# The last low part of h*y on VectorE between the residual adds, and sequence 0 projected bank by bank

## The reference

```python
x = L0_attn_x
xn = _layernorm(x, axis=-1)
x = x + _L0_attn_ref(xn, ...) + _L0_ffn_ref(xn, ...)

# _L0_attn_ref: a gated linear recurrence
y = gelu(xn @ w_y + b_y)
conv = causal 4-tap convolution over time of (xn @ w_x + b_x), plus conv_b
gate_x, gate_a = sigmoid(conv @ w_ig + b_ig), sigmoid(conv @ w_ag + b_ag)
a = exp(-8 * gate_a * softplus(a_param));  mult = sqrt(1 - a * a)   # 0 and 1 at t = 0
h[t] = a[t] * h[t-1] + gate_x * conv * mult
out = (h * y) @ w_out + b_out

# _L0_ffn_ref: ternary weights q(w) = clip(round(w / s), -1, 1) * s with s = mean(abs(w))
out = (silu(xn @ q(w1).T) * (xn @ q(w3).T)) @ q(w2).T
```

## Time and profile before

| | before |
|---|---|
| median of 3 runs | 72.7 us (72.6 to 72.8) |
| profiled execution | 72.7 us |
| its span | 70.9 us |
| TensorE matmuls busy | 67.0 us, 95% |
| VectorE busy | 56.5 us, 80% |
| ScalarE busy | 52.1 us, 73% |
| GpSimd busy | 42.4 us, 60% |
| granted TensorE clock | 1.00 |

### The profile page before, as it was taken

The page is one execution under the profiler, slowest core; times in us unless marked ns, Lnnn a source line. Parts: engine busy times, 40 slices in busy tenths (PEclk is TensorE's granted clock), DMA queues, the critical chain, the costliest instruction groups (busy, mean ns, idle before and its releaser), DMA issues.

```text
span 70.9 us, 1026 instructions
## 1 busy us (share of the span) xinstructions
PE 67.0 (95%) x327; PEld 56.2 (79%) x327; DVE 56.5 (80%) x100; ACT 52.1 (73%) x80; POOL 42.4 (60%) x57
## 2 busy tenths in 40 slices
PE   4999999999999999999999999999999999999940
PEld 4998898877888888888888888888888889987630
DVE  0098898999999999999939964198976999996660
ACT  3395798599989999999989768989969961333000
POOL 6577874799996591000000899678796698566300
PEclk9999999999999999999999999999999999999999
DMA  0899999999000000000000000000000000000564
GB/s 0 293 226 320 393 400 404 389 340 359 18 0 0 5 0 0 0 0 0 0 5 0 5 0 9 0 0 0 0 0 0 0 0 0 0 0 0 191 246 155
DMA packets 4021, 6.66 MB, mean 94 GB/s; under 512 B 476, under 2 KB 1456, under 8 KB 4016
## 3 DMA queue, kind: packets, MB, share of 16 engines
q1 hardware_dynamic: 3728, 6.46, 25.6%
q10 hardware_dynamic: 288, 0.14, 0.7%
HBM read 5.56 MB, written 1.05 MB: 93 GB/s over the span
## 4 chain that ended last, share of the span: by engine, by line
PE 66%; DVE 10%; POOL 5%; issue 5%; ACT 4%; DMA 4%; POOLq 2%; DVEq 0%
PE slot L790 26%; PE slot L773 24%; DVE slot L668 5%; PE slot L853 4%; PE slot L886 4%; DMA par<-params 4%; PE slot L821 3%; PE slot L799 3%; PE slot L762 2%; POOL rstd L271 2%; DVE slot L657 2%; POOLq L52 2%; POOL conv_lo L347 2%; ACT L462 2%; DVE tx L674 1%
## 5 line engine op out<-in xcount | busy, mean ns | idle before, releaser
L301 POOL TENSOR_TENSOR g_lo<-w_raw,g_hi 128x512 fp32r<-128x512 f32 x10 | 12.9, 1303 | 14.6 <-DVE tx L641 12.3
L790 PE MATMUL slot<-xt_hi,w_q 128*128 128x512 f32 x40 | 15.7, 393 | 0.0
L790 PE MATMUL slot<-xt_lo,w_q 128*128 128x512 f32 x40 | 15.7, 393 | 0.0
L629 DVE SCALAR_TENSOR_TENSOR w_raw<-w_raw,s,slot 128x512 f32<-128x512 f32 x10 | 7.4, 747 | 4.9 <-ACT w_raw L407 4.9
L607 DVE SCALAR_TENSOR_TENSOR conv<-slot,par,conv 128x511 f32<-128x511 f32 (+2 forms) x12 | 9.0, 748 | 0.4
L790 PEld LDWEIGHTS slot<-xt_lo,w_q 128*128 128x128 f32 x40 | 7.5, 188 | 1.7
L790 PEld LDWEIGHTS slot<-xt_hi,w_q 128*128 128x128 f32 x40 | 7.5, 188 | 1.7
L407 ACT ACTIVATE w_raw<-slot,scale 128x512 f32<-128x512 f32 x10 | 6.8, 689 | 2.4 <-PE slot L790 2.3
L811 PE MATMUL slot<-g_hi,w_q 128*128 128x512 f32 (+1 forms) x25 | 8.3, 346 | 0.0
L811 PE MATMUL slot<-g_lo,w_q 128*128 128x512 f32 (+1 forms) x25 | 8.2, 346 | 0.0
L293 POOL TENSOR_TENSOR conv_lo<-conv,conv_hi 128x512 fp32r<-128x512 f32 x4 | 5.9, 1473 | 1.5 <-ACT conv_hi L428 1.4
(11 more groups left out here) (127 smaller groups left out, 164.8 us busy)
## 6 DMA issues: line engine op xcount, KB each, us to landing
w_raw<-w13t SPq DMA_DIRECT2D x2, 682.0 KB, 7.4
w_raw<-dense SPq DMA_DIRECT2D x5, 256.0 KB, 5.5
x_both<-x SPq DMA_DIRECT2D x4, 256.0 KB, 4.0
x_both<-xt SPq DMA_DIRECT2D x2, 512.0 KB, 5.3
out<-x_both SPq DMA_DIRECT2D x3, 256.0 KB, 2.1
w_raw<-w2t SPq DMA_DIRECT2D x1, 640.0 KB
out<-x_both ACTq DMA_DIRECT2D x1, 128.0 KB, 2.0
out<-x_both SPq DMA_DIRECT2D x1, 128.0 KB, 1.7
```

Source lines behind the costliest of these rows:

```text
L301: nc.gpsimd.tensor_tensor(g_lo[:, j, s], g[:, n % RING], g_hi[:, j, s].bitcast(f32), ALU.subtract).then_inc(g_lo_set, 1)
L629: nc.vector.scalar_tensor_tensor(out=g[:, n % RING], in0=silu[:, n % RING], scalar=s32[:, 0:1], in1=slot[H_SLOT[s][j]][:, 1], op0=ALU.mult ...
L790: mm = nc.tensor.matmul(slot[H_SLOT[s][j]][:, o], w13_q[:, c, col:col + P], v[:, s, c], start=(c == 0 and v is xt_hi), stop=(c == KC - 1 a ...
```

## The change

GpSimd makes three of the four low parts of h*y, all but the last (sequence 1, chunk 1). That one is made by VectorE (`last_hy_lo`), between the residual adds 0 and 1, with a semaphore of its own, on which TensorE waits for the terms that read it. TensorE projects sequence 0 one bank after the other, as it does sequence 1: all six terms of bank 0, then all six of bank 1.

```diff
--- before.py
+++ after.py
@@ -180,7 +180,7 @@
             sem("h_psum"), sem("silu_set"), sem("g_set"), sem("g_hi_set"), sem("g_lo_set"))
         t_psum, silu_t_set, g_t_set, gt_hi_set, gt_lo_set = (
             sem("t_psum"), sem("silu_t_set"), sem("g_t_set"), sem("gt_hi_set"), sem("gt_lo_set"))
-        hy_hi_set, hy_lo_set = sem("hy_hi_set"), sem("hy_lo_set")
+        hy_hi_set, hy_lo_set, hy_lo_last_set = sem("hy_hi_set"), sem("hy_lo_set"), sem("hy_lo_last_set")
         o_psum, o_set = sem("o_psum"), sem("o_set")
 
         ON_ACT = FULL + 1
@@ -341,10 +341,10 @@
 
             for c in range(KC):
                 gated_products(c)
-            for s in range(SEQS):
-                for c in range(KC):
-                    pool.wait_ge(hy_hi_set, KC * s + c + 1)
-                    nc.gpsimd.tensor_tensor(hy_lo[:, s, c], tx[:, s, c], hy_hi[:, s, c].bitcast(f32), ALU.subtract).then_inc(hy_lo_set, 1)
+            for n in range(SEQS * KC - 1):
+                s, c = divmod(n, KC)
+                pool.wait_ge(hy_hi_set, n + 1)
+                nc.gpsimd.tensor_tensor(hy_lo[:, s, c], tx[:, s, c], hy_hi[:, s, c].bitcast(f32), ALU.subtract).then_inc(hy_lo_set, 1)
 
 
         @block.scalar
@@ -673,6 +673,12 @@
                 dve.wait_ge(h_set, KC * s + c + 1)
                 nc.vector.tensor_tensor(tx[:, s, c], state(s, c), y[:, s, c], ALU.mult).then_inc(hy_set, 1)
 
+            def last_hy_lo():
+
+                s, c = SEQS - 1, KC - 1
+                dve.wait_ge(hy_hi_set, SEQS * KC)
+                nc.vector.tensor_tensor(hy_lo[:, s, c], tx[:, s, c], hy_hi[:, s, c].bitcast(f32), ALU.subtract).then_inc(hy_lo_last_set, 1)
+
             def output(n):
 
                 s, i = O_ALL[n]
@@ -748,7 +754,9 @@
                         gated_products(c)
                     scan(s, c)
                     gated_output(s, c)
-            for n in range(len(O_ALL)):
+            output(0)
+            last_hy_lo()
+            for n in range(1, len(O_ALL)):
                 output(n)
 
 
@@ -815,7 +823,10 @@
 
                 for c in range(KC):
                     for k, (v, w, ready) in enumerate(((hy_hi, w_hi, hy_hi_set), (hy_hi, w_lo, hy_hi_set), (hy_lo, w_hi, hy_lo_set))):
-                        pe.wait_ge(ready, KC * s + c + 1)
+                        if v is hy_lo and KC * s + c + 1 == SEQS * KC:
+                            pe.wait_ge(hy_lo_last_set, 1)
+                        else:
+                            pe.wait_ge(ready, KC * s + c + 1)
                         for i in banks:
                             o, cols, bank = O_PARTS[s][i]
                             mm = nc.tensor.matmul(bank[:, 0:cols.stop - cols.start], w[:, WOUT, c, o * P:(o + 1) * P], v[:, s, c, cols],
@@ -925,9 +936,9 @@
             pe.wait_ge(g_hi_end_set, 2 * FULL - 1 - ON_ACT)
             down(1)
             pe.wait_ge(wout_lo_set, 1)
-            project(0, range(len(O_PARTS[0])))
-            for i in range(len(O_PARTS[1])):
-                project(1, [i])
+            for s in range(SEQS):
+                for i in range(len(O_PARTS[s])):
+                    project(s, [i])
 
 
 def kernel(L0_attn_x, L0_attn_w_y, L0_attn_b_y, L0_attn_w_x, L0_attn_b_x, L0_attn_conv_w, L0_attn_conv_b,
```

## The result

The changed kernel takes 72.41 us in the median of 20 runs, the kernel before 72.74 in as many; the ratio is 0.9949 with a 95% interval of 0.9934 to 0.9965, so it is faster by 0.5%. The profiled execution took 72.29 us with a span of 70.5.

The account below looks back on a forecast made before the run. TensorE, busy 95% of the span, was taken as the bound, with a late hole of 0.41 us and the tail behind its last matmul. Closing the hole: 72.7 - 0.41 = 72.29, so 72.3 us; range 72.1 to 72.6.

Parts of the forecast that it names:

- The hole on TensorE: Late projection matmuls: TensorE's wait for the last low part of h*y costs 0.41 us, and all of it goes.
- Bank order at nothing: Sequence 0's projection: six extra waits and the new order cost nothing; bank 0 can be read at 63.67 us.
- The subtraction on VectorE: Last low part: starts at 64.90, takes 0.69 us, ready at 65.59 instead of 66.20; up to 65.79 costs nothing.
- VectorE as the bound: Residual adds at the end: VectorE's own shortest chain ends at 67.72 us, 0.63 us away from being the bound.
- The tail: Last store: the queue is empty when it comes, so its 1.7 us from issue to landing stay.
- Rival B: End of kernel: no measurable gain, as TensorE meets another hole or the stores' tail absorbs it; 72.5 to 72.8 us, chance 0.15.
- Rival C: VectorE's subtraction ends later than GpSimd's did, after 66.20; with a 1.06 us lock loss 73.15 us, chance 0.06.
- The sum: Whole kernel: 72.7 less 0.41 us gives 72.29, so 72.3 us, 0.56% less.

Follow-up runs that it names:

- the run with other data: The kernel before, with the last low terms of sequence 1 reading chunk 0's low part instead of chunk 1's; 72.49 us, ratio 0.9938.
- The run in which GpSimd reads: The changed kernel with one more GpSimd subtraction of 128x512 (result unused) behind its last one; 72.83 us, ratio 0.9982 to the kernel before.

## Why the prediction was right

**The hole on TensorE.** 0.41 us predicted from the spacing of matmuls, 0.41 found: the last starts at 67.48, to the hundredth. Reading the hole from the weight load's wait, 0.57, would have been wrong by 0.16, and the run with other data shows that 0.41 is all that there is.

**Bank order at nothing.** The matmuls keep their pace with the six waits more, and the early low part that bank 0 wants is there in time. The step was right in cost and in worth: it lets residual add 0 go ahead of the subtraction without making it late. The other way to have the subtraction in time, ahead of the adds, meets the store tail, which takes 0.3 of the 0.41 us. The prediction didn't weigh that order. The early first store has no worth of its own, as the run with other data shows. I had the store times right (64.9, 66.3, 67.2, 67.7 and 68.4 predicted; 64.84, 66.24, 67.22, 67.67 and 68.37 found).

**The subtraction on VectorE.** 0.69 us taken, 0.69 found. I took 0.08 us from the rounding's end to its start; it was 0.04, so it started at 64.86 and not 64.90. By the runs with a late subtraction its slack to TensorE is 0.2 us, as worked out.

**VectorE as the bound.** It still waits 0.23 us ahead of adds 2 and 4, and one instruction of 0.61 us more doesn't make it the bound.

**The tail.** 1.7 us from the last issue to landing, as before. Rival B had 0.15. Its mechanism is real but isn't met in this order. That the queue is empty I had worked out with 370 GB/s for stores 2 and 3. At 317 GB/s, the other rate in the earlier trace rows, they would have ended at 69.29, behind the 69.2 of the last store, so the step was less safe than it reads. The trace has the engines at 93% from 68.05 to 69.65, with the dip to 59% from 69.10 to 69.30: the queue is only just empty.

**Rival C** was decided, as I wrote, by where VectorE's subtraction ends. The run in which GpSimd reads brought it about: 0.53 us lost, half of the 1.06 that I had taken from 25.6 us, because GpSimd had 0.67 us left when VectorE's began and not 1.24; in both places the loss is what GpSimd had left, less 0.14 to 0.19. It was 0.28 us slower than the changed kernel, though not slower than the one before.

**The sum.** 72.3 predicted. The profiled execution took 72.29 and the median of 20 runs is 72.41, since some executions are displaced at the start. The median of the kernel before moved to 72.74 with more runs too, so the difference measured is 0.33 to 0.37 us for the 0.41 of the trace. The ratio's interval allows 0.25 to 0.48, so this doesn't speak against 0.41. That the forecast of 72.3 is 0.11 below the median comes from the displaced executions, which it hadn't reckoned with.

## What to carry to other kernels

Read a hole on TensorE from the starts of the matmuls around it, not from the wait of its weight load, and find the latest arrival that costs nothing; both come from one row. Two edits can each be worth nothing and together be worth all, when one shortens a step and the other lets it start: ask of a faster engine what it stands behind. When work is put off to let something urgent go first, look at the stores that it feeds. The kernel with the subtraction first had TensorE and VectorE end at the same time as the better one and still ended 0.3 us later.

## What the runs showed of the hardware

- A VectorE subtraction with two SBUF inputs took 1.22 us beside a GpSimd subtraction and 0.69 beside a GpSimd memset; GpSimd's subtraction took 1.30, as it does alone. The time held up stands in the VectorE instruction's own duration, with no wait shown ahead of it.
- VectorE started 0.04 us after ScalarE's result, and GpSimd 0.08 after the same.
- GpSimd's addition of a column of biases in place took 1.58 us for 128x512, more than its subtraction of two tensors (1.30).
- Stores of 1.05 MB in one piece ran at 355 GB/s, and the last of them took 2.0 us from issue to landing instead of 1.7.
